# The load back of the quarter sums behind the next group's first adding load, with all engines' lists drawn anew

## The chip, the cores and the metric

One core of a Trainium2 chip runs the whole kernel. The metric is the device time of one execution in microseconds. The profile gives the span of one profiled execution, from its first to its last instruction.

## The reference

`x` is (64, 12, 224, 224) float32, 154 MB. Every 16x16 patch of every channel is summed, which gives 196 tokens of 12 numbers for each image, and a 12x192 matrix makes the embeddings. Then follow a layer norm with attention over 12 heads, and a layer norm with a two-layer network (192 to 768 to 192, gelu), each added to its input:

```python
pooled = x.reshape(Bb, Cc, n, K, n, K).sum(axis=(3, 5))
out = jnp.einsum('bcij,ce->bije', pooled, channel_weights)
...
_, idx = jax.lax.top_k(selection[..., 0], k_sel)
gated = attn_output * selection
src = jnp.take_along_axis(gated, idx[..., None], axis=1)
y = jax.vmap(lambda xb, ib, sb: xb.at[ib].add(sb))(x, idx, src)
...
h = h + _L0_attn_ref(_layernorm(h, axis=-1), ...)
h = h + _L0_ffn_ref(_layernorm(h, axis=-1), ...)
```

The attention writes to the 14 tokens with the highest selection only, so attention queries are needed for 14 tokens of each image.

## The kernel before

The 64 images are worked on in 16 groups of four. Each engine runs a list of steps, `plan`, once per period; there are 20 periods. A step is written stage:step:lag, and in period p it works on group p minus lag. Lags are counted for each engine by itself. What an engine does is done in the order of its list, and the engines wait for each other by semaphores. The steps that matter here:

- **Loading and summing.** The group's input is seven tiles X0 to X6. SyncE loads tile t of the next group as soon as VectorE has summed tile t of this one. Tiles 1, 3 and 5 are loaded whole. Of tiles 0, 2, 4 and 6 SyncE loads one half, and GpSimd issues a second transfer that adds the other half to it (`X:t`, an adding load, line 344). VectorE sums a tile in `L:t` (line 892) into R.
- **Quarter sums.** When L:6 is done, GpSimd stores R to memory (`R:st`, line 391), loads it back in another shape once the store has landed (`R:ld`, line 397), and adds four quarters up into P with three instructions (`P:s`, lines 353 to 360). TensorE's `A:tm` (line 482) takes P.
- **Token statistics.** VectorE's `A:var`, `A:log`, `A:var2` (two reciprocal square roots by iteration), then `A:sel`, `A:top` (the 14 chosen tokens), `A:slots`. ScalarE's `A:e` gives the exponentials that `A:sel` needs.
- **Chosen tokens.** `G:ga`, `G:u` and `S:sc` (scores), ScalarE's exponentials `S:e0` to `S:e5` and scalings `S:n`, VectorE's `S:ri`, then `S:et`, `S:g`, `S:at`. Their feed forward `C:xh`, `C:xt`, `C:fa`, `C:fb`, `C:f2`, `C:os` is done for two groups together in every second period. GpSimd stores the result by index (`c:s`, line 367).
- **Feed forward of all tokens.** `K:*` makes stacked low-precision parts, `f:n` are 12 first-layer matmuls with a gelu each, and `o:i.m` second-layer matmuls of seven token tiles in three pieces. `O:i` on ScalarE copies a tile out.

GpSimd's transfers (adding loads, store, load back, `c:s`) go through one software queue; SyncE's loads go through a queue of their own.

Of the kernel before, what the change touches and what calls it, by code (L numbers as in the profile page):

```python
# [5 lines left out]
B, C, IMG, PATCH, D, HEADS, HID = 64, 12, 224, 16, 192, 12, 768  # L6
# [100 lines left out]
def program(nc, x, cw, wqkv, bqkv, selw, selb, ow, ob, temp, w1t, b1, w2, consts, e48, e13r, out):  # L107
# [9 lines left out]
    with ExitStack() as ctx:  # L117
        def sb(name, shape, dt=f32):
            return ctx.enter_context(nc.sbuf_tensor(name, shape, dt))
# [7 lines left out]
        K = sb("K", [128, NCOLS])  # L127
# [22 lines left out]
        X = [sb(f"X{k}", [128, TQ * QB // (2 if k in ADDED else 1)]) for k in range(XT)]  # L150
        R = sb("R", [128, 2, NQ * N])
        Praw = sb("Praw", [BC, 2, NQ * 128 * N // BC])
        Pt = sb("Pt", [BC, 2, T])
        P = [sb(f"P{i}", [PF, T]) for i in range(2)]
# [3 lines left out]
        sc = {n: sb(n, [HALF, 2 * GB]) for n in ("var", "lr", "L", "t1", "t2", "s2", "den", "rden")}  # L158
# [9 lines left out]
        v26, d1, d2 = (sb(n, [HALF, 4 * GB, W1]) for n in ("v26", "d1", "d2"))  # L168
# [16 lines left out]
        h1, xh = sb("h1", [PROWS, D]), sb("xh", [PROWS, D])  # L185
        bst, mv = sb("bst", [PROWS, 6]), sb("mv", [PROWS, 2])
        XH = sb("XH", [DH + 1, 2, ROWS])
# [152 lines left out]
        def _(pool):  # L340
# [55 lines left out]
                    by_itself(pool)  # L396
                    pool.dma_start(Praw[:, r, :], sums_in[bass.ds(g, 1)].rearrange("o p q -> (o p) q")).then_inc(sums_back[r], 16)

            plan = ("X:2:1 P:s:2 X:4:1 K:v:2 K:d1:2 X:6:1 K:d2:2 X:0:0 R:st:1 R:ld:1 c:s:4").split()

            def body(i, k):
                for what in plan:
# [19 lines left out]
        def _(pe):  # L422
# [173 lines left out]
            def step_F2(g, u, i, m):  # L596
# [9 lines left out]
                else:  # L606
# [1 line left out]
                        pe.wait_ge(act_K.sem, act_K.at(g, "k2"))  # L608
                    pe.matmul(to, Stk2[u % 2][:, i * OT:(i + 1) * OT], RS[:, :], start=False, stop=True).then_inc(pe_F2.sem, 1)  # L609

            plan = ("o:1.2:2 o:2.0:2 o:2.1:2 o:2.2:2 o:3.0:2 o:3.1:2 o:3.2:2 K:tr1:1 S:et:2 f:0:1 K:tr2:1 o:4.0:2 "
                    "o:4.1:2 S:g:2 A:sl:1 f:1:1 o:4.2:2 f:2:1 at:0:2 f:3:1 at:1:2 at:2:2 f:4:1 o:5.0:2 f:5:1 A:st:1 "
                    "o:5.1:2 f:6:1 G:ga:1 f:7:1 o:5.2:2 f:8:1 G:u:1 f:9:1 A:tm:0 o:6.0:2 C:xt:2 f:10:1 S:sc:1 "
                    "o:6.1:2 C:fa:2 o:6.2:2 A:zt:0 f:11:1 C:fb:2 o:0.0:1 o:0.1:1 o:0.2:1 C:f2:2 o:1.0:1 o:1.1:1").split()

            def body(i, k):
                for what in plan:
# [23 lines left out]
        def _(act):  # L641
# [90 lines left out]
            def step_F2(g, u, i):  # L732
# [4 lines left out]
                if i == FT - 1:  # L737
# [1 line left out]
                    act.dma_start(og[bass.ds(g, 1)].rearrange("o p q -> (o p) q"),  # L739
                                  obuf[u % 2][:, :, :].rearrange("p i e -> p (i e)")).then_inc(y_out[u % 2], 16)  # L740

            plan = ("S:e1:2 O:0:2 S:e2:2 K:M:1 S:e3:2 S:e4:2 S:e5:2 O:1:2 K:L:1 S:n:2 K:k1:1 O:2:2 S:t:2 K:k2:1 "
                    "f:0:1 O:3:2 f:1:1 f:2:1 f:3:1 f:4:1 f:5:1 f:6:1 O:4:2 f:7:1 O:5:2 f:8:1 G:rs:1 f:9:1 f:10:1 "
                    "C:XH:2 C:ga:2 O:6:2 f:11:1 A:fm:0 C:gb:2 A:e:0 K:H:0 S:e0:1").split()

            def body(i, k):
                for what in plan:
# [18 lines left out]
        def _(dve):  # L766
# [294 lines left out]
            def prepare(t):  # L1061
# [12 lines left out]
                elif t == 6:  # L1074
                    for m in range(3):
                        weights_heads(m)

            plan = ("A:slots:2 L:0:0 G:ga:2 C:xh:3 G:u:2 A:var:1 A:log:1 A:var2:1 S:sc:2 L:1:0 L:2:0 A:sel:1 S:ri:2 "
                    "L:3:0 L:4:0 L:5:0 L:6:0 S:g:2 A:top:1 C:os:3 S:at:2").split()

            def body(i, k):
                for what in plan:
# [50 lines left out]
```

## Time and profile before

| | |
|---|---|
| runs | 807.29, 798.75, 805.67 us, median 805.67 |
| profiled execution | 803.36 us, of which the span is 801.8 us |
| busy | TensorE 642.9 us (80%), VectorE 531.2 (66%), ScalarE 337.8 (42%), GpSimd 175.3 (22%) |
| mean granted clock of TensorE | 0.845 of full speed |
| moved | 172.55 MB, mean 215 GB/s |

Busy time counts instructions in flight on an engine, not waits. The DMA share is the time that packets took, divided over 16 DMA engines; as packets of several queues overlap it can read above 1. The granted clock reads 1.0 for 2.4 GHz and 0.5 for 1.2 GHz.

### The profile page before, as it was taken

What the parts mean: (1) busy time and instruction counts of PE and PEld (TensorE: products, weight loads), DVE (VectorE), ACT (ScalarE), POOL (GpSimd) and SP (SyncE); (2) the same over time, 40 slices, a digit from 0 to 9 for tenths busy, and PEclk for the clock granted to TensorE, in tenths of its full rate; (3) what the DMA queues carried; (4) which work ended last, traced back from release to release, by engine and by line L of the source; (5) the groups of instructions that cost most, each with busy time, mean ns of one, the idle gap of its engine ahead of it and who ended that gap; (6) DMA issues with size and microseconds to landing.
All of it is one profiled execution on the core that took longest, in us unless ns stands there. A gap on an engine that the chain in (4) does not pass through costs nothing. (4 is left out here: it accounts for less than half of the span.)

```text
span 801.8 us, 12223 instructions
## 1 busy us (share of the span) xinstructions
PE 642.9 (80%) x3860; PEld 528.7 (66%) x3860; DVE 531.2 (66%) x1357; ACT 337.8 (42%) x826; POOL 175.3 (22%) x244
## 2 busy tenths in 40 slices
PE   0353279696988979886989888897989799899996
PEld 0152158584967768675968677675968588688775
DVE  0865849486767876686668764795668767677312
ACT  0000317272553617272555526472555427275651
POOL 1102222222223112322232112322232112311000
PEclk9996558798896959797797959996797959799999
DMA  9996898969696969889596959888597969620011
GB/s 311 322 314 144 234 271 221 277 188 310 170 322 135 320 143 292 241 236 283 168 316 168 328 122 288 237 261 245 159 317 176 333 126 333 143 52 31 5 32 35
DMA packets 64589, 172.55 MB, mean 215 GB/s; under 512 B 4456, under 2 KB 54824, under 8 KB 58378
## 3 DMA queue, kind: packets, MB, share of 16 engines
q1 hardware_dynamic: 32512, 110.11, 37.5%
q0 software_dynamic: 27648, 49.55, 34.0%
q10 hardware_dynamic: 4362, 12.07, 4.4%
q8 instruction: 33, 0.54, 0.3%
q14 instruction: 34, 0.28, 0.1%
HBM read 158.99 MB, written 12.73 MB: 214 GB/s over the span
## 5 line engine op out<-in xcount | busy, mean ns | idle before, releaser
L605 PE MATMUL psO<-W,act 128*112 128x192 f32 x1344 | 283.9, 359 | 14.1 <-ACT act L729 9.1
L892 DVE TENSOR_REDUCE R<-X 128x42 f32<-128x1344 f32 (+1 forms) x112 | 235.3, 2140 | 36.6 <-DMA X<-in_x 36.3
L605 PEld LDWEIGHTS psO<-W,act 128*112 128x112 f32 x1344 | 237.2, 195 | 32.2 <-ACT act L729 14.0
L729 ACT ACTIVATE act<-psF 128x392 f32<-128x392 f32 x192 | 95.4, 497 | 188.3 <-PE psF L593 183.4
L344 POOL DMA_DIRECT2D X<-in_x x64 | 85.2, 1331 | 40.6 <-DMA X<-in_x 33.8
L593 PE MATMUL psF<-Stk,M1S 104*128 104x392 bf16 x192 | 70.6, 368 | 5.1 <-ACT act L729 4.2
L736 ACT ACTIVATE obuf<-psO 112x192 f32<-112x192 f32 x112 | 36.2, 323 | 65.0 <-PE psO L609 64.7
L544 PE MATMUL psS<-FM,UB 64*112 64x196 f32 x192 | 62.1, 503 | 0.1
L482 PE MATMUL psA<-TMR,P 49*98 49x108 f32 x64 | 14.8, 376 | 57.5 <-POOL P L360 57.5
L544 PEld LDWEIGHTS psS<-FM,UB 64*112 64x112 f32 x192 | 51.5, 279 | 10.6 <-issue 8.0
L482 PEld LDWEIGHTS psA<-TMR,P 49*98 49x98 f32 x64 | 10.8, 245 | 62.0 <-POOL P L360 54.8
L391 POOL DMA_DIRECT2D patch_sums<-R x16 | 10.0, 622 | 168.2 <-DVE R L892 157.8
L702 ACT ACTIVATE Sm<-Sm,nm 112x196 f32<-112x196 f32 x96 | 42.5, 444 | 8.3 <-issue 4.6
L918 DVE COPY F<-psA 98x216 f32<-98x216 f32 x16 | 6.1, 381 | 58.1 <-PE psA L482 58.1
L565 PE MATMUL psS<-B,G 128*56 128x192 f32 x192 | 38.5, 339 | 6.7 <-DVE G L1028 6.7
L556 PE MATMUL psS<-ET,F 98*64 98x336 f32 x128 | 39.6, 452 | 0.2 <-ACT ET L711 0.2
L593 PEld LDWEIGHTS psF<-Stk,M1S 104*128 104x128 bf16 x192 | 20.1, 104 | 29.7 <-ACT act L729 12.8
L707 ACT ACTIVATE Sm<-Sm,rinv 112x196 f32<-112x196 f32 x96 | 35.1, 447 | 1.3 <-DVE rinv L1023 1.3
L580 PEld LDWEIGHTS psC<-XH,W1T 97*128 97x128 f32 x192 | 34.4, 265 | 0.4 <-ACT actS L723 0.2
L565 PEld LDWEIGHTS psS<-B,G 128*56 128x56 f32 x192 | 22.7, 131 | 17.2 <-DVE G L1028 10.0
L580 PE MATMUL psC<-XH,W1T 97*128 97x112 f32 x192 | 34.0, 348 | 0.0
L1028 DVE TENSOR_TENSOR G<-psS,K 64x336 f32<-64x336 f32 x32 | 16.0, 499 | 26.9 <-PE psS L556 26.4
(192 smaller groups left out, 906.1 us busy)
## 6 DMA issues: line engine op xcount, KB each, us to landing
X<-in_x SPq DMA_DIRECT2D x48, 1344.0 KB, 10.1
X<-in_x SPq DMA_DIRECT2D x64, 672.0 KB, 10.5
X<-in_x POOLq DMA_DIRECT2D x64, 672.0 KB, 9.7
out<-obuf ACTq DMA_DIRECT2D x16, 588.0 KB, 3.6
patch_sums<-R POOLq DMA_DIRECT2D x16, 147.0 KB, 6.4
Praw<-patch_sums POOLq DMA_DIRECT2D x16, 147.0 KB, 5.7
W1T<-in_w1t ACTq DMA_DIRECT2D x1, 576.0 KB
W<-in_w ACTq DMA_DIRECT2D x1, 576.0 KB
```

The lines of the kernel that those rows point to most:

```text
L344: pool.dma_start(half_tile(t), half_rows(g, t, 1), accum_op=ALU.add).then_inc(x_added[t], 16)
L544: mm = pe.matmul(psS[0:ROWS, j // 2, (j % 2) * T:(j % 2 + 1) * T], UB[:, j, :, :].rearrange("p k s -> p (k s)"), FM[r][:, :], start=True, ...
L556: mm = pe.matmul(psS[0:ZR, 1 + i, 0:3 * ROWS], F[r][:, k, 0:ZR], ET[:, k * HP + 3 * i:k * HP + 3 * i + 3, :].rearrange("p j s -> p (j s)") ...
L565: mm = pe.matmul(psS[0:SLOTS, 0, 0:D], G2[:, j, :], B2[:, j, :], start=(j == 0), stop=(j == HP - 1))
L580: mm = pe.matmul(psC[:, (h % HA) * ROWS:(h % HA + 1) * ROWS], W1T[bias_first(k), k, h * 128:(h + 1) * 128], XH[bias_first(k), k, :], start ...
L593: pe.matmul(psF[:, 0:GT // 2], M1S[:, (n // 2) * 128:(n // 2 + 1) * 128], Stk1[u % 2][:, (n % 2) * (GT // 2):(n % 2 + 1) * (GT // 2)], sta ...
L605: pe.matmul(to, act_sb[u % 2][:, m, i * OT:(i + 1) * OT], W2[:, m, :], start=(m == 0), stop=False)
L702: act.activation(Sm[:, j, :], Sm[:, j, :], ACT.Exp, bias=nm[:, j:j + 1], accum_out=rsum[:, j:j + 1]).then_inc(act_S.sem, 1)
L707: act.activation(Sm[:, j, :], Sm[:, j, :], ACT.Copy, scale=rinv[:, j:j + 1]).then_inc(act_S.sem, 1)
L729: act.activation(act_sb[u % 2][:, n // 2, (n % 2) * (GT // 2):(n % 2 + 1) * (GT // 2)], psF[:, 0:GT // 2], ACT.Gelu).then_inc(act_F1.sem, 1)
L736: act.activation(obuf[u % 2][:, i, :], psO[(i + u) % 2][0:OT, 0:D], ACT.Copy).then_inc(act_F2.sem, 1)
L892: dve.tensor_reduce(R[:, r, t * TQ * N:(t + 1) * TQ * N].rearrange("p (q j) -> p q j", q=TQ), v, AX.XY, ALU.add).then_inc(dve_L, 1)
```

## The change

The load back of the quarter sums, `R:ld`, stands no longer right behind `R:st` but in the next period behind `X:2` (so its lag is 2 where it was 1). The lists of all engines are drawn anew. Nothing is computed otherwise, no instruction is added or taken out, and no buffer changes.

```diff
 # GpSimd
-            plan = ("X:2:1 P:s:2 X:4:1 K:v:2 K:d1:2 X:6:1 K:d2:2 X:0:0 R:st:1 R:ld:1 c:s:4").split()
+            plan = ("X:2:1 R:ld:2 X:4:1 P:s:2 X:6:1 X:0:0 K:v:2 K:d1:2 K:d2:2 R:st:1 c:s:4").split()
 # TensorE
-            plan = ("o:1.2:2 o:2.0:2 o:2.1:2 o:2.2:2 o:3.0:2 o:3.1:2 o:3.2:2 K:tr1:1 S:et:2 f:0:1 K:tr2:1 o:4.0:2 "
-                    "o:4.1:2 S:g:2 A:sl:1 f:1:1 o:4.2:2 f:2:1 at:0:2 f:3:1 at:1:2 at:2:2 f:4:1 o:5.0:2 f:5:1 A:st:1 "
-                    "o:5.1:2 f:6:1 G:ga:1 f:7:1 o:5.2:2 f:8:1 G:u:1 f:9:1 A:tm:0 o:6.0:2 C:xt:2 f:10:1 S:sc:1 "
-                    "o:6.1:2 C:fa:2 o:6.2:2 A:zt:0 f:11:1 C:fb:2 o:0.0:1 o:0.1:1 o:0.2:1 C:f2:2 o:1.0:1 o:1.1:1").split()
+            plan = ("o:1.2:2 o:2.0:2 o:2.1:2 o:2.2:2 o:3.0:2 K:tr1:1 o:3.1:2 S:et:2 o:3.2:2 K:tr2:1 f:0:1 S:g:2 "
+                    "f:1:1 A:sl:1 o:4.0:2 f:2:1 o:4.1:2 at:0:2 f:3:1 at:1:2 at:2:2 f:4:1 A:st:1 o:4.2:2 f:5:1 G:ga:1 "
+                    "f:6:1 o:5.0:2 o:5.1:2 f:7:1 G:u:1 o:5.2:2 C:xt:2 A:tm:0 o:6.0:2 C:fa:2 f:8:1 S:sc:1 f:9:1 "
+                    "o:6.1:2 f:10:1 o:6.2:2 f:11:1 C:fb:2 o:0.0:1 o:0.1:1 o:0.2:1 o:1.0:1 A:zt:0 C:f2:2 o:1.1:1").split()
 # ScalarE
-            plan = ("S:e1:2 O:0:2 S:e2:2 K:M:1 S:e3:2 S:e4:2 S:e5:2 O:1:2 K:L:1 S:n:2 K:k1:1 O:2:2 S:t:2 K:k2:1 "
-                    "f:0:1 O:3:2 f:1:1 f:2:1 f:3:1 f:4:1 f:5:1 f:6:1 O:4:2 f:7:1 O:5:2 f:8:1 G:rs:1 f:9:1 f:10:1 "
-                    "C:XH:2 C:ga:2 O:6:2 f:11:1 A:fm:0 C:gb:2 A:e:0 K:H:0 S:e0:1").split()
+            plan = ("S:e1:1 S:e2:1 S:e3:1 O:0:1 S:e4:1 K:H:0 S:e5:1 K:M:0 A:fm:0 O:1:1 K:L:0 S:n:1 O:2:1 A:e:0 "
+                    "K:k1:0 S:t:1 K:k2:0 f:0:0 f:1:0 f:2:0 f:3:0 O:3:1 f:4:0 f:5:0 O:4:1 f:6:0 f:7:0 C:XH:1 G:rs:0 "
+                    "O:5:1 C:ga:1 f:8:0 f:9:0 f:10:0 O:6:1 f:11:0 C:gb:1 S:e0:0").split()
 # VectorE
-            plan = ("A:slots:2 L:0:0 G:ga:2 C:xh:3 G:u:2 A:var:1 A:log:1 A:var2:1 S:sc:2 L:1:0 L:2:0 A:sel:1 S:ri:2 "
-                    "L:3:0 L:4:0 L:5:0 L:6:0 S:g:2 A:top:1 C:os:3 S:at:2").split()
+            plan = ("C:os:4 A:sel:2 L:0:0 L:1:0 S:g:3 A:top:2 S:at:3 A:slots:2 L:2:0 G:ga:2 C:xh:3 L:3:0 G:u:2 "
+                    "A:var:1 S:sc:2 A:log:1 A:var2:1 L:4:0 L:5:0 S:ri:2 L:6:0").split()
```

## Rows read from the trace of the kernel before

**Rows 1.** From `L391` among the rows of the tile patch_sums: GpSimd's 16 stores

```profile
L391 POOL DMA_DIRECT2D patch_sums<-R x16: 616/622/627, 63.4 to 716.0; - x16
```

**Rows 2.** The page: TensorE's busy time, and the two large DMA queues

```profile
PE 642.9 (80%) x3860; PEld 528.7 (66%) x3860; DVE 531.2 (66%) x1357; ACT 337.8 (42%) x826; POOL 175.3 (22%) x244
...
q1 hardware_dynamic: 32512, 110.11, 37.5%
q0 software_dynamic: 27648, 49.55, 34.0%
```

**Rows 3.** Windows: stretch, length, busy of PE, PEld, DVE, ACT, POOL; clock, DMA, GB/s

```profile
338.00:341.00 3.00, 3.00 (x10) 2.44 (x10) 2.64 (x12) 0.00 (x0) 0.80 (x3) 0.50 0.08 13
...
359.00:362.00 3.00, 2.04 (x11) 1.23 (x11) 2.45 (x10) 0.99 (x2) 0.62 (x1) 1.00 1.03 344
...
708.00:752.00 44.00, 43.82 (x311) 36.77 (x310) 26.85 (x86) 28.02 (x67) 4.76 (x10) 1.00 0.10 28
```

**Rows 4.** Timeline of GpSimd: start, length, instruction, idle before and its releaser

```profile
317.43 0.62 POOL L391 DMA_DIRECT2D patch_sums<-R  x1 [8.86 <-DVE R L892]
324.10 0.55 POOL L397 DMA_DIRECT2D Praw<-patch_sums  x1 [6.05 <-DMA patch_sums<-R]
...
330.28 0.53 POOL L353 TENSOR_TENSOR Pt<-Praw 48x196 f32<-48x196 f32 x1 [1.46 <-DMA Praw<-patch_sums]
...
359.94 0.62 POOL L391 DMA_DIRECT2D patch_sums<-R  x1 [9.59 <-DVE R L892]
```

**Rows 5.** Timeline of TensorE in the same period

```profile
313.78 0.55 PE L510 MATMUL psA<-identb,SP 98*104 98x98 bf16 x8
...
332.13 1.03 PE L482 MATMUL psA<-TMR,P 49*98 49x108 f32 x4 [3.43 <-POOL P L360]
...
334.97 4.26 PE L544 MATMUL psS<-FM,UB 64*112 64x196 f32 x12
```

**Rows 6.** Timeline of VectorE in the same period

```profile
318.12 1.03 DVE L1028 TENSOR_TENSOR G<-psS,K 64x336 f32<-64x336 f32 x2 [1.52 <-PE psS L556]
...
323.99 1.54 DVE L892 TENSOR_REDUCE R<-X 128x42 f32<-128x1344 f32 x1
325.44 0.21 DVE L992 TENSOR_TENSOR ZY<-psS,K 112x56 f32<-112x56 f32 x1
...
328.01 0.91 DVE L1007 TENSOR_TENSOR UB<-psS,K 64x336 f32<-64x336 f32 x2 [1.82 <-PE psS L529]
333.20 0.38 DVE L918 COPY F<-psA 98x216 f32<-98x216 f32 x1 [4.28 <-PE psA L482]
...
340.09 1.38 DVE L1014 TENSOR_TENSOR Sm<-psS,RM 112x1176 f32<-112x1176 f32 x1
...
343.00 4.40 DVE L892 TENSOR_REDUCE R<-X 128x42 f32<-128x2688 f32 x2
```

**Rows 7.** Timeline of ScalarE: the six scalings S:n

```profile
349.82 2.19 ACT L707 ACTIVATE Sm<-Sm,rinv 112x196 f32<-112x196 f32 x6
```

**Rows 8.** The chain that ended last: first and last instruction of a C:xh

```profile
785.30 0.37 DVE bst L1044
...
788.20 0.39 DVE xh L1052
```

**Rows 9.** Rows of the tile Praw: landing of all 16 load backs

```profile
DMA to landing us min/median/max: 2.7/5.7/6.4
```

**Rows 10.** Two adding loads (line 344) issued one behind the other, and their landings

```profile
L344 POOL DMA_DIRECT2D X<-in_x x1: 1294/1294/1294, 346.5 to 346.5; - x1
...
DMA to landing us min/median/max: 11.0/11.0/11.0
...
L344 POOL DMA_DIRECT2D X<-in_x x1: 1299/1299/1299, 349.1 to 349.1; - x1
...
DMA to landing us min/median/max: 16.8/16.8/16.8
```

**Rows 11.** Instructions of line 482 (A:tm): the matmuls, with first and last start

```profile
L482 PE MATMUL psA<-TMR,P x64: 252/384/497, 73.4 to 726.6; 49*98 49x108 f32 x64
```

## The prediction

> **What bounds the kernel now.** I began with the instruction that marks a period, GpSimd's store of R. Its sixteen issues run from 63.4 to 716.0 us [rows 1], so a period lasts 652.6 / 15 = 43.5 us; 63 us of filling lie ahead of the first and 86 us of draining behind the last. No engine fills such a period. TensorE is the busiest, with 642.9 us [rows 2], but part of that is work at half clock. In the drain 311 matmuls took 43.82 us at full clock [rows 3], 0.141 us each; by that the 3860 of the whole kernel, 241 a period, are 34 us of a period. The two big DMA queues take 37.5 and 34.0% of 801.8 us [rows 2]; the other 12.9 of the 172.55 MB, at the first queue's rate of 110.11 MB in 37.5%, take 4.4%. Together that is 609 us, or 38.0 us a period.
>
> So next I followed one period through the timelines. T is the end of L:6. In the period that starts with the store at 317.43 the store lands after 6.7 us, the load back lands some 6 us later, and the quarters are added from 330.28 [rows 4]. TensorE starts A:tm at 332.13 after 3.43 us of idleness, so it was ready at 328.7 [rows 5]. VectorE, which stands in front of A:var and has nothing else that it may do, waits 4.28 us, starts at 333.20, is through with A:var, A:log and A:var2 at 340.09 and with S:sc at 343.00 [rows 6]. Only then come L:1 and L:2 (4.40 us), A:sel, S:ri and L:3 to L:6 with 8.8 us by the same lengths (1.5 us for a small tile, 2.9 for a large one), and the store of the next group at 359.94. Every piece of this waits for the one before: **the round trip through memory and VectorE's list in series are the loop that sets the period**, here 42.5 us.
>
> Two costs hang on this loop. After the idle stretch at A:tm the granted clock is 0.50 and is still so at 338 to 341 [rows 3]; S:sc takes 4.26 us for 12 matmuls [rows 5]. And the DMA engines, at 1.03 in 359 to 362, stand at 0.08 in 338 to 341 [rows 3], since no tile has been summed for so long. Both are losses, and not yet the bound.
>
> **The change part by part.** Cyclically, VectorE's list keeps its token and attention steps mostly in order. What is moved is the tile sums against them: before, A:var stood behind L:0; after, it stands behind L:3, and A:sel, S:g, A:top, S:at, A:slots, G:ga and G:u stand between L:6 and it.
>
> (a) *Cover for the round trip.* Between L:6 and A:var stand now: A:sel 0.7, L:0 1.5, L:1 2.9, the steps from S:g to A:slots 5.1 (from 318.12 to 323.99, less 0.7 of C:os), L:2 1.5, G:ga 0.8, L:3 2.9, G:u 0.9 [rows 6], in sum 16.3 us. One new wait enters: A:sel needs ScalarE's A:e, which now stands behind the six scalings of S:n (2.19 us, [rows 7]), and these wait for S:ri, which stands just ahead of L:6. S:n, a copy and A:e are about 2.8 us from S:ri, L:6 covers 1.5, so VectorE stands 1.3 us. Queued behind it are L:0 and all that follows, so I count it in full: A:var is reached at T + 17.6. In every second period C:xh adds 3.3 us [rows 8] and C:os 0.7, which fits into the wait: T + 20.9. TensorE comes to A:tm at about the same time: S:et waits for S:n until T + 1, takes 1.3, a piece of o 0.7, and from K:tr2 to the end of what stands ahead of A:tm TensorE took 14.9 us before (313.78 to 328.70, [rows 5]) with nearly the same contents; that is T + 18.
>
> (b) *The round trip itself.* The store is issued as before, at T + 0.8, and lands 6 to 7 us later. Into that wait comes X:2, whose first half was loaded long ago, so its 1.3 us of issuing are covered. In every second period c:s stands ahead of it (two issues, 2.5 us, behind C:os). The load back is issued at T + 7.6. But it is now behind an adding load in the software queue, and what a transfer pays for that, the trace of before doesn't show for this pair. Bound from below: nothing, it lands after 5.7 us as in the median now [rows 9], at T + 13.3. Bound from above: the adding load that was issued 2.6 us behind another landed 16.8 us after its issue instead of 11.0, that is 8.4 us behind the other's landing [rows 10]; a load back that fared as badly would land at T + 24.4. It moves 147 KB instead of 672, and its quickest landing took 2.7 us [rows 9], so I take X:2's landing (issue at T + 1.7 plus 11.0 as the first of the pair) and 2 to 3 us on top: T + 15.5, 17.5 in periods with c:s. P is ready 1.8 us later, T + 17.3 or 19.3, against 17.6 to 20.9 when it is asked for: the round trip is hidden, with hardly a microsecond to spare.
>
> The Trainium skill (page DMA: Bandwidth & Descriptors, section on queues, rings and completion order) says that each DMA engine takes the descriptors of one ring in order and goes round the rings packet by packet. By that rule the load back starts behind all of X:2; without it the load back would land at T + 13.3, the period would be no shorter, as A:var's place decides. The pair of adding loads agrees with the rule.
>
> (c) *X:2 for L:2.* Before, X:2 was issued behind the load back (324.10, [rows 4]) and asked for at 345.9 (the second of the sums from 343.00, [rows 6]), with some 18 us between; now L:2 is reached at T + 12.9, and X:2 lands at T + 12.7 (16 with c:s, and later where the store ahead holds it up). I charge 1 us in the one kind of period and 3 in the other. X:4 is issued at T + 8.3, X:6 and X:0 behind P:s at T + 18 and later; they are needed a period later, and if each takes 8.4 us behind the other they land by T + 26, 34 and 42. L:0 of the next period comes at about T + 42. That too is tight.
>
> (d) *From A:tm to the next L:6.* A:tm 1.0, A:var to A:var2 6.9, S:sc 2.9 [rows 6], L:4, L:5, S:ri and L:6 6.1: 16.9 us. The scores matmuls are done while A:var runs, if the clock is full. C:fa is covered by A:var in part.
>
> (e) *Sum of the loop.* 17.6 + 16.9 = 34.5 and 20.9 + 16.9 = 37.8, mean 36.2 us; with (c) 38.2. That is also what the DMA engines need (38.0). Two chains that long, both nearly full and coupled at X:2, X:0 and the load back, don't run at their mean: the same walk for the period shown (store 7.5, load back 6.2, quarters 1.8, A:tm 1.0, statistics 6.9, S:sc 2.9, L:1 and L:2 4.4, A:sel and S:ri 0.9, L:3 to L:6 8.8) gives 40.4 us where 42.5 stand, and the mean is 43.5. I add 1.8 us and take **40.0 us**. TensorE (34 us of work) then idles for 6 us a period, in short pieces at K:tr1, S:et and C:xt, so I count on a full clock most of the time.
>
> (f) *The ends.* Filling stays at 63 us: it is loading and weights. Draining gets longer. Before, A:tm of the last group started 11 us behind L:6 (726.6 at the latest of its matmuls, [rows 11], against 716.0); now it stands behind G:u and o:5.2 of the groups before, which TensorE reaches at T + 18 by (a), less about 1 us since VectorE has no tiles to sum. What follows A:tm is the same work. I add 6 us: 86 becomes 92.
>
> Against the profiled execution: 63.4 + 15 x 40.0 + 92 = 755.4 of span, plus 1.6 around it, **757 us**. This execution (803.36) lies 0.3% under the median of 805.67, and I leave it at that.
>
> **The rivals.** *The load back really is late* (slower). Its place: GpSimd's queue. If it fares like the second adding load, P is ready at T + 26.2 and TensorE idles 8 us at A:tm, after which it runs at half clock, as now. Then A:tm ends at 27.2, the scores come at 32.5, S:sc and the statistics end at 38.8, L:4 to L:6 at 44.9: a period of 45 us and 63.4 + 675 + 92 + 1.6 = 832 us. It decides from a landing about 5 us later than mine. For it speaks the pair of adding loads, against it the size. Chance 0.15.
>
> *DMA engines and tiles as the bound.* The transfers are spread better but the tiles arrive late, VectorE waits at L:2, L:0 and L:6, and the period is 42 us: 787 us. For it speaks that 38.0 us is already 87% of the present period; against it that the engines stand idle for 8 us of this one. Chance 0.13.
>
> *The gain is eaten* by new short waits (A:sel, K:tr1 behind K:L, the coupled period) and the longer drain: a period of 43.3 us, 806 us. Chance 0.09.
>
> *Everything fits* and the period is 37.5 us: 720 us. Chance 0.07.
>
> **How the numbers follow.** My forecast, 757 us (periods of 38.5 to 41.5 us, 734 to 780), has 0.56. The range reaches from 728 to 812: it leaves out most of the best case, and most of the slow one. No measurement of this kernel can tell less than about 1% from no change. Faster by over 1% is the forecast, the DMA case and the best case, 0.75; within 1% 0.09; slower 0.16.
>
> **What would show it.** The stores of R would follow each other at about 40 us. TensorE's idle time that P releases (3.43 us in the period shown) would be under 1 us, and the clock over 0.9 where it is 0.845 in the mean. The DMA share would have no trough like 0.08. The load back would land later than now behind its issue. VectorE would show a wait of about 1.3 us for A:e ahead of A:sel, and one for X at L:2. The last store to the end would be 92 us. I would be wrong if P is late and the clock falls, if X:2 or X:0 hold VectorE for more than 3 us, or if the drain grows by far more than 6 us.

## The result, and the profile after

| | before | after |
|---|---|---|
| runs, median | 804.79 us (4 runs, 798.75 to 807.29) | 741.18 us (4 runs, 740.7 to 743.38) |
| span of the profiled execution | 801.8 us | 741.8 us |
| mean granted clock of TensorE | 0.845 | 0.886 |

The ratio is 0.9225, 95% interval 0.917 to 0.928: 7.7% faster. Some executions of this kernel run in a slower state, so every ratio here and below is of the fast ones alone, while the times are medians of all (and the profile of one run below, with `A:sel` behind `L:0`, is of such a slow execution, as is that of the run with `X:2` in front of the store and `c:s` kept).

First the marks of the periods, the stores of R (rows of the tile patch_sums, of after), which answer to [rows 1], and the landing of all load backs, which answers to [rows 9]:

```profile
L391 POOL DMA_DIRECT2D patch_sums<-R x16: 612/624/630, 63.9 to 648.4; - x16
...
DMA to landing us min/median/max: 2.8/7.1/10.0
```

Filling ends at 63.9 us as before, fifteen periods take 584.5 us (38.97 each, before 43.5), and draining takes 741.8 - 648.4 = 93.4 us (before 86). The fifteen are not alike: the ten between the stores at 203.88 and 613.99 take **41.0 us** each (before, between those at 228.39 and 674.70, 44.6), while the first four and the last take 34.9 on average (before 41.3).

The page of after, for [rows 2]:

```profile
PE 612.1 (83%) x3860; PEld 494.7 (67%) x3860; DVE 535.2 (72%) x1357; ACT 340.4 (46%) x826; POOL 176.2 (24%) x244
...
q1 hardware_dynamic: 32512, 110.11, 41.7%
q0 software_dynamic: 27648, 49.55, 35.8%
```

The periods are of two kinds. GpSimd's timeline of after shows one of each (start, length, instruction, idle before and releaser), for [rows 4], between the first and the last of those stores:

```profile
203.88 0.63 POOL L391 DMA_DIRECT2D patch_sums<-R  x1 [3.10 <-DVE R L892]
...
285.74 0.62 POOL L391 DMA_DIRECT2D patch_sums<-R  x1 [3.10 <-DVE R L892]
286.78 1.00 POOL L367 DMA_INDIRECT out<-OS,idx  x1 [0.42 <-issue]
...
289.02 1.48 POOL L344 DMA_DIRECT2D X<-in_x  x1
292.59 0.59 POOL L397 DMA_DIRECT2D Praw<-patch_sums  x1 [2.10 <-DMA patch_sums<-R]
...
302.39 0.54 POOL L353 TENSOR_TENSOR Pt<-Praw 48x196 f32<-48x196 f32 x1 [7.81 <-DMA Praw<-patch_sums]
...
328.87 0.62 POOL L391 DMA_DIRECT2D patch_sums<-R  x1 [0.86 <-DVE R L892]
330.07 1.29 POOL L344 DMA_DIRECT2D X<-in_x  x1 [0.58 <-issue]
336.34 0.58 POOL L397 DMA_DIRECT2D Praw<-patch_sums  x1 [4.98 <-DMA patch_sums<-R]
...
343.73 0.53 POOL L353 TENSOR_TENSOR Pt<-Praw 48x196 f32<-48x196 f32 x1 [5.43 <-DMA Praw<-patch_sums]
...
368.00 0.62 POOL L391 DMA_DIRECT2D patch_sums<-R  x1 [3.09 <-DVE R L892]
...
613.99 0.63 POOL L391 DMA_DIRECT2D patch_sums<-R  x1 [3.18 <-DVE OS L1059]
```

The period from 285.74 holds c:s and lasts 43.1 us; the one from 328.87 holds C:xh instead and lasts 39.1. What VectorE does in both (timeline of after, for [rows 6]): the sum of tile 2, the first instruction of A:var, in the first kind S:sc, and between the two the first instruction of A:sel, which waits for ScalarE's A:e:

```profile
301.52 1.55 DVE L892 TENSOR_REDUCE R<-X 128x42 f32<-128x1344 f32 x1 [4.67 <-DMA X<-in_x]
...
309.41 0.38 DVE L918 COPY F<-psA 98x216 f32<-98x216 f32 x1 [1.85 <-PE psA L482]
...
315.48 1.38 DVE L1014 TENSOR_TENSOR Sm<-psS,RM 112x1176 f32<-112x1176 f32 x1 [2.52 <-PE psS L544]
...
331.04 0.17 DVE L949 TENSOR_TENSOR den<-Ex 98x8 f32<-98x8 f32 x1 [3.01 <-ACT Ex L666]
...
341.75 1.54 DVE L892 TENSOR_REDUCE R<-X 128x42 f32<-128x1344 f32 x1
...
351.42 0.36 DVE L918 COPY F<-psA 98x216 f32<-98x216 f32 x1
```

And TensorE (timeline of after, for [rows 5]): G:u, A:tm and S:sc of the first kind, A:tm and S:sc of the second:

```profile
303.35 2.53 PE L529 MATMUL psS<-ZY,A 64*64 64x56 f32 x24 [3.50 <-DVE ZY L992]
...
308.34 1.03 PE L482 MATMUL psA<-TMR,P 49*98 49x108 f32 x4
...
311.18 4.26 PE L544 MATMUL psS<-FM,UB 64*112 64x196 f32 x12
...
348.27 0.61 PE L482 MATMUL psA<-TMR,P 49*98 49x108 f32 x4
...
351.58 2.24 PE L544 MATMUL psS<-FM,UB 64*112 64x196 f32 x12
```

A:tm no longer waits for P in either: P is there at 304.2 and TensorE comes at 308.3 in the first kind, at 345.5 and 348.3 in the second. In the first kind the wait has moved: tile 2 is 4.67 us late, G:u is 3.50 us late behind it, and after that TensorE runs at half clock, with S:sc at 4.26 us as before. Windows of after, for [rows 3] (columns as there):

```profile
300.00:303.00 3.00, 0.00 (x0) 0.00 (x0) 1.48 (x2) 0.38 (x1) 0.61 (x2) 1.00 1.15 232
309.00:312.00 3.00, 3.00 (x11) 2.10 (x10) 2.25 (x12) 0.50 (x1) 0.00 (x0) 0.50 1.16 223
...
317.00:320.00 3.00, 2.25 (x8) 1.54 (x6) 2.75 (x12) 1.14 (x3) 0.00 (x0) 0.50 0.13 22
...
351.00:354.00 3.00, 3.00 (x20) 2.50 (x19) 2.66 (x14) 0.93 (x2) 0.00 (x0) 1.00 1.14 204
```

### The profile page after: what moved, and what is told of

The parts are those of the page before. It is cut to its first block, busy times and chain, and to the rows that moved or that the text cites. A ratio compares the mean times of both kernels' runs of the same rounds, so it can differ in the third digit from the quotient of the medians.

```text
span 741.8 us, 12238 instructions
## 1 busy us (share of the span) xinstructions
PE 612.1 (83%) x3860; PEld 494.7 (67%) x3860; DVE 535.2 (72%) x1357; ACT 340.4 (46%) x826; POOL 176.2 (24%) x244
## 3 DMA queue, kind: packets, MB, share of 16 engines
q0 software_dynamic: 27648, 49.55, 35.8%
## 4 chain that ended last, share of the span: by engine, by line
PE 26%; DVE 22%; DMA 21%; issue 19%; ACT 6%; POOL 3%; ACTq 2%; POOLq 1%; DVEq 0%
DMA X<-in_x 10%; PE psO L605 9%; DVE R L892 7%; DMA OB<-in_ob 5%; DMA Praw<-patch_sums 4%; DMA patch_sums<-R 3%; PE psS L565 2%; PE psS L544 2%; PE psF L593 2%; PE psS L529 2%; DVE mx L1018 2%; DVE Sm L1014 2%; ACT Sm L707 2%; PE psS L550 2%; ACT L729 1%
## 5 line engine op out<-in xcount | busy, mean ns | idle before, releaser
L605 PEld LDWEIGHTS psO<-W,act 128*112 128x112 f32 x1344 | 226.5, 188 | 32.1 <-ACT act L729 17.4
L375 POOL TENSOR_TENSOR v<-F,t 98x96 f32<-98x96 f32 x16 | 5.4, 339 | 212.2 <-DVE y_ln L906 212.2
L736 ACT ACTIVATE obuf<-psO 112x192 f32<-112x192 f32 x112 | 35.8, 320 | 27.8 <-PE psO L609 27.6
L544 PE MATMUL psS<-FM,UB 64*112 64x196 f32 x192 | 48.0, 412 | 0.0
L529 PE MATMUL psS<-ZY,A 64*64 64x56 f32 x384 | 32.2, 252 | 18.2 <-DVE ZY L992 18.1
L529 PEld LDWEIGHTS psS<-ZY,A 64*64 64x64 f32 x384 | 30.0, 165 | 23.6 <-issue 23.6
L544 PEld LDWEIGHTS psS<-FM,UB 64*112 64x112 f32 x192 | 40.4, 222 | 7.4 <-issue 5.2
L593 PEld LDWEIGHTS psF<-Stk,M1S 104*128 104x128 bf16 x192 | 19.8, 103 | 37.8 <-ACT act L729 20.5
L679 ACT ACTIVATE SP<-v 98x624 bf16<-98x624 f32 x16 | 11.6, 726 | 63.4 <-POOL v L378 63.4
L1014 DVE TENSOR_TENSOR Sm<-psS,RM 112x1176 f32<-112x1176 f32 x16 | 22.1, 1380 | 18.8 <-PE psS L544 18.8
L556 PEld LDWEIGHTS psS<-ET,F 98*64 98x64 f32 x128 | 16.2, 136 | 22.3 <-ACT ET L711 8.3
## 6 DMA issues: line engine op xcount, KB each, us to landing
X<-in_x POOLq DMA_DIRECT2D x64, 672.0 KB, 12.5
```

Source lines behind the costliest of these rows:

```text
L529: mm = pe.matmul(psS[0:ZR, 1 + h // HP, (h % HP) * SLOTS:(h % HP + 1) * SLOTS], A4[:, h, :], ZY[0:ZR, :], start=True, stop=True)
L544: mm = pe.matmul(psS[0:ROWS, j // 2, (j % 2) * T:(j % 2 + 1) * T], UB[:, j, :, :].rearrange("p k s -> p (k s)"), FM[r][:, :], start=True, ...
L556: mm = pe.matmul(psS[0:ZR, 1 + i, 0:3 * ROWS], F[r][:, k, 0:ZR], ET[:, k * HP + 3 * i:k * HP + 3 * i + 3, :].rearrange("p j s -> p (j s)") ...
L593: pe.matmul(psF[:, 0:GT // 2], M1S[:, (n // 2) * 128:(n // 2 + 1) * 128], Stk1[u % 2][:, (n % 2) * (GT // 2):(n % 2 + 1) * (GT // 2)], sta ...
L605: pe.matmul(to, act_sb[u % 2][:, m, i * OT:(i + 1) * OT], W2[:, m, :], start=(m == 0), stop=False)
L1014: dve.tensor_tensor(Sm[:, :, :].rearrange("p (k j) t -> p k j t", k=3), psS[0:ROWS, :, 0:2 * T].rearrange("p k (j t) -> p k j t", j=2), RM ...
```

## The experiments

All ratios are to the kernel before, run on the same chip beside each. T is the end of L:6, as in the prediction.

### One half of the change each

*The load back moved, all other engines' lists as before.*

```diff
-            plan = ("X:2:1 P:s:2 X:4:1 K:v:2 K:d1:2 X:6:1 K:d2:2 X:0:0 R:st:1 R:ld:1 c:s:4").split()
+            plan = ("X:2:1 R:ld:2 P:s:2 X:4:1 K:v:2 K:d1:2 X:6:1 K:d2:2 X:0:0 R:st:1 c:s:4").split()
```

> The kernel before, with one part of the change alone: the load back R:ld stands behind X:2 of the next period, all else (P:s, c:s and the lists of the other engines) as before. If the lists of the other engines carry the gain (my theory): the load back now queues behind an adding load and lands at about T + 14.7 (7.1 us after its issue, as in the kernel after) instead of T + 13.3; the round trip is not covered here, so each of 15 periods gets 1.5 to 4 us longer: 825 to 860 us. Rival, that the gain comes from the move of the load back itself (X:2 is issued 6 us earlier, GpSimd doesn't stand waiting): 745 to 785 us.

Measured: 858.8 us, ratio 1.066 (1.060 to 1.072). TensorE's waits for P from 200 to 700 us (total, times, longest), in this run and in the kernel before:

```profile
PE psA L482 <- POOL P L360: 79.1, 10, 9.0
...
PE psA L482 <- POOL P L360: 37.0, 10, 5.7
```

P is late, as expected. Part of it is not the queue: c:s now stands ahead of X:2 and the load back and waits for C:os, which in the old VectorE list comes some 6 us after L:6, so in such periods the load back is issued at T + 10.

*The load back put back, all other lists as after.*

```diff
-            plan = ("X:2:1 R:ld:2 X:4:1 P:s:2 X:6:1 X:0:0 K:v:2 K:d1:2 K:d2:2 R:st:1 c:s:4").split()
+            plan = ("X:2:1 X:4:1 P:s:2 X:6:1 X:0:0 K:v:2 K:d1:2 K:d2:2 R:st:1 R:ld:1 c:s:4").split()
```

> The kernel after, with the load back put back right behind its store (R:st:1 R:ld:1 c:s:4), all other lists as after. GpSimd then waits 6 to 7 us for the store before it may issue X:2. My theory: P is ready some 2 us earlier, which nobody waits for, but X:2 is issued at T + 8.5 (11 with c:s) and lands 9 to 11 us later, while VectorE asks for it at T + 12.9: a wait of 5 to 9 us at L:2 in every period, TensorE idle ahead of G:u and at half clock after it: periods of 44 to 46 us, 810 to 845 us. Rival, that the lists of the other engines carry the whole gain and the place of the load back is indifferent: 735 to 750 us.

Measured: 840.5 us, ratio 1.042 (1.037 to 1.047). VectorE's waits from 200 to 700 us, where after has 24.2 us in 6 waits for X and 14.3 in 6 for S:sc:

```profile
DVE R L892 <- DMA X<-in_x: 72.7, 11, 8.2
DVE Sm L1014 <- PE psS L544: 37.2, 11, 5.5
```

So neither half is worth anything alone: each costs 4 to 7%, together they bring 7.7%. The lists need X:2 early, and the load back can only stand behind it where the lists cover the round trip.

### The round trip by itself

*Before, without the wait for the store.* The load back fetches the sums stored one period earlier, so the tokens are those of the group before; bytes and instructions are the same.

```diff
-                    pool.wait_ge(sums_out[r], landed(g, r))
+                    pool.wait_ge(sums_out[1 - r], landed(g - 1, 1 - r))
...
-                    pool.dma_start(Praw[:, r, :], sums_in[bass.ds(g, 1)]...
+                    pool.dma_start(Praw[:, r, :], sums_in[bass.ds(g - 1, 1)]...
```

> The kernel before, but the load back fetches the sums that were stored one period earlier (so the tokens are those of the group before), with as many bytes and instructions; it needn't wait for the store that was just issued. The 6.7 us of waiting go out of the round trip, nothing else changes. My theory (round trip and VectorE's list in series set the period): P is ready 5 to 6 us earlier, TensorE doesn't idle at A:tm, periods of 38 to 40 us: 735 to 765 us. Rival (the DMA engines, or another chain, set the period before as well): 785 to 806 us.

Measured: 726.0 us, ratio 0.899 (0.891 to 0.906), periods of 38.3 us. That is a larger gain than the 735 to 765 us that I expected. The round trip did set the period before.

*The same edit in the kernel after.*

> The kernel after, with the load back fetching the sums that were stored one period earlier, as in the run on the kernel before (tokens are those of the group before). It takes the same 6.7 us wait out. My theory: in the kernel after the round trip is covered, P is ready 4 us ahead of A:tm; nothing waits for it: 725 to 745 us, of which a gain could only come from X:4 and later transfers being issued earlier. Rival (the round trip still sets the period): 690 to 715 us.

Measured: 737.8 us, ratio 0.918 (0.911 to 0.925), nothing against after's 0.9225. The round trip sets nothing any more. This run also shows the queue. The adding load X:2 was issued at 287.1 and the load back, which now waits for nothing, at 288.0 (rows of line 344 and of the tile Praw):

```profile
L344 POOL DMA_DIRECT2D X<-in_x x1: 1476/1476/1476, 287.1 to 287.1; - x1
...
DMA to landing us min/median/max: 12.4/12.4/12.4
```

```profile
L402 POOL DMA_DIRECT2D Praw<-patch_sums x1: 1182/1182/1182, 288.0 to 288.0; - x1
...
DMA to landing us min/median/max: 13.1/13.1/13.1
```

The load back of 147 KB landed at 301.1, 1.6 us behind X:2 (299.5); its median landing is 5.7 us with nothing in front of it [rows 9]. The rule of the Trainium skill that each DMA engine takes the descriptors of one ring in order (page DMA: Bandwidth & Descriptors, section on queues, rings and completion order) agrees with this.

### The late tile

*After, with c:s behind the load back.* All engines run one more period at the end, for c:s of the last pair.

```diff
-            plan = ("X:2:1 R:ld:2 X:4:1 P:s:2 X:6:1 X:0:0 K:v:2 K:d1:2 K:d2:2 R:st:1 c:s:4").split()
+            plan = ("X:2:1 R:ld:2 c:s:5 X:4:1 P:s:2 X:6:1 X:0:0 K:v:2 K:d1:2 K:d2:2 R:st:1").split()
-END = NG + 4
+END = NG + 5
```

> The kernel after, with the store by index c:s moved in GpSimd's list from ahead of X:2 to behind R:ld (lag 5, and one more period at the end for all engines). In the trace of after, periods with c:s last 43.3 us and the others 38.6; in the former VectorE waits 4.67 us for X:2 at L:2, TensorE idles 3.5 us ahead of G:u and runs at half clock for 20 us. My theory: that is the 2.5 us by which c:s delays X:2; without it these five periods come to 39 or 40 us: 718 to 730 us. Rival, that these periods are longer because of C:xh, C:fa, C:fb and C:f2, or that the DMA engines are full anyway: 736 to 746 us.

Measured: **696.1 us, ratio 0.862 (0.856 to 0.868)**, the fastest kernel of all. Its stores:

```profile
L391 POOL DMA_DIRECT2D patch_sums<-R x16: 610/626/628, 63.2 to 599.7; - x16
```

A period is 35.8 us. GpSimd's timeline of this run has the two kinds again:

```profile
347.34 0.62 POOL L391 DMA_DIRECT2D patch_sums<-R  x1 [3.10 <-DVE R L892]
348.01 1.28 POOL L344 DMA_DIRECT2D X<-in_x  x1
...
381.75 0.63 POOL L391 DMA_DIRECT2D patch_sums<-R  x1 [3.09 <-DVE R L892]
...
419.82 0.63 POOL L391 DMA_DIRECT2D patch_sums<-R  x1 [3.31 <-DVE R L892]
```

The kind with c:s fell from 43.1 to 34.4 us, the other from 39.1 to 38.1. The gain is larger than I expected: 8.7 us in such a period, of which the late tile is 4.7. VectorE's waits for X from 200 to 600 us are 4.3 us in 8, none over 1.0, and the mean clock is 0.953. In the kernel after itself, the last period has c:s ahead of X:2 too, but no tiles of a next group are loaded any more: X:2, issued at 617.1, lands after 8.2 us, VectorE doesn't wait for it, and the period lasts 34.4 us at a DMA share of 0.60. So it is c:s and full DMA engines together that make the tile late.

*The half clock by itself.* Ten matmuls whose result is overwritten keep TensorE busy in front of the wait, first before A:tm in the kernel before, then before G:u of every second group in the kernel after:

```diff
+                        for _ in range(10):
+                            pe.matmul(psA[0:OT, 0:D], kc("ident")[:, 0:OT], W2[:, 0, :], start=True, stop=True)
                     pe.wait_ge(pool_P.sem, pool_P.at(g, "p"))
...
+                    if u % 2:
+                        for _ in range(10):
+                            pe.matmul(psS[0:OT, 1, 0:D], kc("ident")[:, 0:OT], W2[:, 0, :], start=True, stop=True)
                     pe.wait_ge(dve_G.sem, dve_G.at(g, "zy"))
```

> The kernel before, with ten extra matmuls (about 3.4 us at full clock, their result is overwritten) on TensorE in front of the wait for P in A:tm, so that the engine doesn't idle there. It tells the price of the half clock apart from that of the wait. My theory: the wait for P stays in the loop, since VectorE still gets A:tm at the same time; only the half clock goes, which in the period shown cost VectorE next to nothing (S:sc was done before VectorE came to it) and in others some 4 us: 770 to 795 us, mean clock over 0.93. Rival (the half clock is what made the kernel before slow, the wait itself is harmless): 730 to 760 us.

> The kernel after, with the same ten extra matmuls in front of G:u in every second group, where TensorE waits 3.5 us for VectorE's L:2 and that for X:2. The late X:2 stays, the half clock goes. The periods with c:s last 43.3 us in the kernel after and 34.3 with c:s behind the load back; the late tile is 4.7 us of these 9. If the half clock is the rest: these periods come to 39 us, 5 of them and part of a sixth, 718 to 726 us, mean clock over 0.93. Rival (the rest is congestion of the DMA engines): 735 to 745 us.

Measured: 798.1 us on before, ratio 0.990 (0.982 to 0.997), clock 0.894: next to nothing, less than I expected, and the clock below the 0.93 that I expected too. The fillers don't keep TensorE busy long enough here, since P comes later than they end. From 200 to 600 us there are still these waits, where before has 27.3 us in 7, and after several of them the clock is 0.50 again:

```profile
PE psA L484 <- POOL P L360: 13.2, 6, 3.4
```

So this run alone doesn't price the half clock in before. Together with the run without the wait for the store it does say which cost is the larger: the two have the same mean clock (0.892 there, 0.894 here) and are 726 and 798 us, so in before the wait itself is the cost.

On after: 736.5 us, ratio 0.911 (0.902 to 0.921), clock 0.932, above the expected 718 to 726, and as a whole not told apart from after's 0.9225 (0.917 to 0.928). The timeline says why (stores of this run):

```profile
285.65 0.62 POOL L391 DMA_DIRECT2D patch_sums<-R  x1 [3.10 <-DVE R L895]
...
324.02 0.62 POOL L391 DMA_DIRECT2D patch_sums<-R  x1 [3.00 <-DVE R L895]
...
362.84 0.62 POOL L391 DMA_DIRECT2D patch_sums<-R  x1 [3.10 <-DVE R L895]
```

The period with c:s is 38.4 us, 4.7 less than in after with the tile as late (4.75 us). So the half clock costs 4.7 us there; VectorE's two waits behind G:u in after, 1.85 us at A:var and 2.52 at S:sc, make 4.4 of it. 4.7 + 4.7 is about the 8.7 of the run with c:s behind the load back. The other periods with c:s gain 4.1 to 5.2 us, but for one (560.6 - 518.4 = 42.3 us) in which the clock fell to 0.50 all the same, with 0.75 us of idleness left at G:u. But the period at 599.7 is 37.8 us where after's last is 34.4, and draining is 96.6 us: where TensorE wasn't waiting, the fillers cost their own 3.4 us.

### Can more be had?

*A:sel behind L:0, on top of the 696 us kernel.*

```diff
-            plan = ("C:os:4 A:sel:2 L:0:0 L:1:0 S:g:3 ...
+            plan = ("C:os:4 L:0:0 A:sel:2 L:1:0 S:g:3 ...
```

> The kernel after with c:s behind the load back (the run that took 696 us), and with A:sel behind L:0 instead of in front of it on VectorE. There VectorE waits about 0.9 us a period at A:sel for ScalarE's A:e. My theory: the loop is now VectorE's own list, so the wait comes off each period: 680 to 690 us. Rival (TensorE or the DMA engines are the bound by now): 692 to 700 us.

Measured: 740.4 us, ratio 0.917 (0.908 to 0.925), against the 0.862 of the 696 us kernel: a step of 1.5 us in one list gave some 44 us back, and neither alternative had that. I had missed that L:2 is then asked for sooner too. VectorE's waits from 200 to 600 us, in an execution of 751.8 us, the longest of the four:

```profile
DVE R L892 <- DMA X<-in_x: 23.9, 10, 4.7
DVE Sm L1014 <- PE psS L544: 18.9, 5, 5.2
DVE G L1028 <- PE psS L556: 12.7, 9, 2.2
```

The wait for A:e became waits for tile 2, S:sc and S:g, and behind idle times of 1.26 to 3.58 us at G:u TensorE was at half clock five times from 250 to 620 us (0.50 in 357 to 369 us behind the one of 1.26).

*X:2 in front of the store,* with c:s behind the load back, with c:s where the change has it, and with A:sel behind L:0:

```diff
+            plan = ("R:ld:2 c:s:5 X:4:1 P:s:2 X:6:1 X:0:0 K:v:2 K:d1:2 K:d2:2 X:2:0 R:st:1").split()
...
+            plan = ("R:ld:2 X:4:1 P:s:2 X:6:1 X:0:0 K:v:2 K:d1:2 K:d2:2 X:2:0 R:st:1 c:s:4").split()
```

> The run that took 696 us (c:s behind the load back), with X:2 in front of R:st instead of behind it (its first half has landed by then). X:2 is issued 4 us ahead of L:6's end instead of 1 us behind it; the store is behind an adding load in the queue. If the landing of X:2 against L:2 is what still loses time here and there: no wait at L:2, 685 to 697 us. Rival (the store is held up by the adding load and P comes late): 700 to 730 us.

> The kernel after, c:s where the change put it, and X:2 in front of R:st. Here c:s delays the load back only, not X:2. If what the kernel after loses against 696 us is the late tile for L:2 (and nothing about c:s as such): 690 to 705 us. Rival (c:s ahead of the load back costs by itself, since it waits for C:os and takes 2.5 us): 720 to 740 us.

> The run with A:sel behind L:0 that took 740 us (there VectorE waited 2.4 us for X at L:2, TensorE idled 1.3 us at G:u and went to half clock), now with X:2 in front of R:st. If the late tile was the cause of its loss: back to 680 to 700 us. Rival (VectorE's new order is bad by itself, the tile wait is a by-product): 725 to 745 us.

Measured: 713.5 us, ratio 0.888 (0.881 to 0.895); 712.4 us, 0.886 (0.877 to 0.895); 721.5 us, 0.897 (0.890 to 0.905). No tile is late in any of them, so the third got back some 16 of the 44 us that A:sel behind L:0 had lost (0.917 to 0.897), and the second, with c:s in its old place, beats after by 29 us. But the store is now the one that stands behind an adding load. First run of the three, landing of the stores of R (line 391), and one of TensorE's A:tm:

```profile
DMA to landing us min/median/max: 2.6/10.5/12.8
...
296.85 0.61 PE L482 MATMUL psA<-TMR,P 49*98 49x108 f32 x4 [1.37 <-POOL P L360]
```

The store lands after 10.5 us in the median instead of 6.5, P is late again (10.1 us in 7 waits from 200 to 600 us), and the place of c:s is indifferent. Behind the four longest of these waits, 1.37 to 2.57 us, the clock is 0.50 for some 7 to 14 us, and VectorE waits 11.2 us in 6 for S:sc, which it never does in the 696 us kernel in that stretch. For the first run the rival came true (700 to 730 us). The second and the third fell between their two alternatives: what they name as the late tile's cost went, and the late store's came in its place.

## Why the prediction was right, and where it was not

**The loop** (round trip and VectorE's list in series) was what bound before: without the wait for the store, 726 us.

**(a) and (b), the cover.** The landing of the load back was given as T + 15.5, 17.5 with c:s. With T at 328.0 and 284.9 it landed at T + 15.7 and 17.5. P was ready 2.7 and 4 us ahead of A:tm. The value was built from X:2's landing and 2 to 3 us more, and that order is shown by the run on after in which the load back waits for nothing. But the parts were off where the sum was right: X:2 landed at T + 11.3 and 16.6 (forecast 12.7 and 16), the load back 4.4 and 0.9 us behind it. That both sums came out to 0.2 us is luck. The bound from above (16.8 us, as for the second adding load) was never reached, so the slow rival didn't come true.

**(a), the wait for A:e,** was given as 1.3 us. It was 0.51 us ahead of the first kind of period and 3.01 ahead of the second; behind the period with the fillers, where the clock held, it was 1.16, so most of the excess is again the half clock.

**(c), the late tile,** was the mis-sized term. I charged 1 us and 3; it was 0 in the periods without c:s and 4.67 with. X:2 was issued at T + 4.1 there, about as assumed, but took 12.5 us to land instead of 11, and L:2 was asked for at T + 12.0, not 12.9. By the prediction's own sign ("if X:2 or X:0 hold VectorE for more than 3 us") this part was wrong, though the time was not. I also added c:s and C:os to the wrong kind of period: they fall into those without C:xh.

**(e), the clock.** "Short pieces, full clock most of the time" failed. The idle time at G:u was 3.50 us in one piece, and the half clock behind it cost 4.7 us in these periods (fillers); the mean clock is 0.886 in the profile and not over 0.9. I had no term for it. The 1.8 us that I added for coupling stood in its place. Measured per kind: 43.1 us with c:s and 39.1 with C:xh. With c:s put where it belongs, (a), (c) and (d) give 37.5 and 38.8; as they stand in the prediction, with c:s and C:xh in one period, 35.5 and 40.8.

**(e), the DMA engines.** "What the DMA engines need (38.0)" was not a least time: the 696 us kernel runs ten whole periods from 202.3 to 565.3, each with all its loads, in 36.3 us. Its window over that stretch:

```profile
202.30:565.30 363.00, 336.31 (x2280) 272.78 (x2280) 320.68 (x805) 210.96 (x515) 110.27 (x150) 1.00 1.02 293
```

The share reads 1.02 there and up to 1.16 in the windows above, so a sum of busy shares can be undercut. It is not far off either, and whether the DMA engines bind the 696 us kernel no run shows. The forecast that the share would have no trough failed as well: it is 0.13 in 317 to 320.

**(a) and (d), the list.** Without the late tile (a) and (d) alone gave 34.5 and 37.8, and the 696 us kernel has 34.4 and 38.1. In part that is luck. A:var starts there at T + 18.5 and 22.1 (17.6 and 20.9 in the prediction), and from it to the next T pass 15.9 and 16.0 us (16.9): the 1.0 us charged for A:tm in (d) isn't there, since A:tm is all but done when VectorE comes to A:var, and about as much was missing in (a).

**(f)** The drain was given as 92 us and took 93.4; filling was 63.9.

In sum 757 us against 741. The mechanism was right, and it is partly luck that the number was near. The mean of fifteen periods was forecast 1.0 us too long, but the ten whole ones last 41.0 us, 1.0 longer than the 40.0: there the half clock and the rest of the late tile cost 2.9 us on top of the 38.2 of (a), (c) and (d), more than the 1.8 allowed for coupling. What made the total smaller than forecast are the five periods at the two ends, 34.9 us on average, for which the prediction had no term of their own.

The signs that came true: from 200 to 700 us P releases no wait of A:tm, the load back lands later behind its issue (7.1 us in the median, before 5.7), VectorE waits for A:e and for X, and the drain is 93.4 us.

What stays open: why TensorE fell to half clock after 1.26 us of idleness in the run with A:sel behind L:0 and after 1.37 at A:tm with X:2 in front of the store, and not after 1.33 us at an o piece in the 696 us kernel; and whether the 4.7 us of half clock would be the same in other places. No run tells that apart.

## What to carry to other kernels

Walk the list of the engine that gates the loop, instruction by instruction, from the release of one buffer to the next: it gave 34.5 and 37.8 us where 34.4 and 38.1 were measured once nothing else was late, with errors of 1 us in its parts that cancelled. Take the mean over whole periods apart from those at the ends, or short periods there will hide long ones in the middle. When transfers share one queue, a change of place is a change for all of them: X:2, the store and the load back can't all be early, and the tight one is found by asking who needs each first. Add a clock term wherever a wait of TensorE is moved, since a wait that moves can take its half clock along, as it did here from A:tm to G:u.

## What the runs showed of the hardware

A small transfer issued behind a large adding load in GpSimd's queue landed behind it: the load back 1.6 us behind X:2 and 13.1 us after its issue (median 5.7 us with nothing ahead), the store after 10.5 us instead of 6.5. In the latter run, with a DMA share of 1.00 over ten whole periods, the load back had no adding load just ahead and landed after 5.3 us in the median. The summed share of the DMA engines read up to 1.16 in 3 us windows while two queues were at work, and 1.02 over ten whole periods of the 696 us kernel.
